# Second attention of a four-layer network: counts, maxima and scores of an iteration put in another order on three engines

## What is computed

```python
def _L1_attn_ref(x, Wq, bq, Wk, bk, Wv, bv, Wo, bo, entropy_ema, entropy_threshold):
    B, L, D = x.shape            # 8 batches of 256 tokens, width 128, 16 heads of 8
    q, k, v = (proj(Wq, bq), proj(Wk, bk), proj(Wv, bv))
    scores = jnp.einsum('bhqd,bhkd->bhqk', q, k) / jnp.float32(np.sqrt(dh))
    attn = jax.nn.softmax(scores, axis=-1)
    sr = MIN_SPARSITY + (1.0 - MIN_SPARSITY) * jax.nn.sigmoid(entropy_ema - entropy_threshold)
    k_keep = jnp.maximum(1, (L * (1.0 - sr)).astype(jnp.int32))
    rank = jnp.argsort(jnp.argsort(-attn, axis=-1), axis=-1)
    w = jnp.where(rank < k_keep[None, :, None, None], attn, jnp.float32(0.0))
    w = w / (jnp.sum(w, axis=-1, keepdims=True) + 1e-10)
    out = jnp.einsum('bhqk,bhkd->bhqd', w, v)
    return out.transpose(0, 2, 1, 3).reshape(B, L, D) @ Wo.T + bo
```

## Time and profile before

| | |
|---|---|
| median of 3 runs | 2033.48 us (2032.08 to 2033.51) |
| the profiled execution | 2029.82 us, its span 2028.1 us |
| busy share of the span | PE 77%, DVE 73%, ACT 55%, POOL 43% |
| second attention, from 480 to 1098 us | 618 us, with DVE busy 538 us, ACT 518 us, PE 421 us, POOL 270 us |

### The profile page before, as it was taken

One profiled execution on the slowest core, in us unless ns is written; L12 is line 12 of the kernel. 1 busy time (PEld: TensorE's weight loads), 2 busy tenths in 40 slices (PEclk: granted clock), 3 DMA queues, 4 the chain that ended last, 5 costly groups with the idle time before them and its releaser, 6 DMA issues.

```text
span 2028.1 us, 38143 instructions
## 1 busy us (share of the span) xinstructions
PE 1561.3 (77%) x12256; PEld 997.2 (49%) x12256; DVE 1480.3 (73%) x4763; ACT 1123.5 (55%) x3354; POOL 877.5 (43%) x1162
## 2 busy tenths in 40 slices
PE   3878989987347777776669788527777799999978
PEld 3445667675223343343336556313443477777763
DVE  6678766555589999999998742458876778887657
ACT  2444444445988998999853333114452377666620
POOL 3333221124244554455333677666200377767610
PEclk8889999997567877878778989758896899999969
DMA  4111101003000000000001033222120000000000
GB/s 139 47 47 43 41 19 43 19 2 123 15 9 17 13 10 12 17 9 9 1 1 59 31 89 106 90 70 69 47 89 1 15 1 1 2 1 2 1 1 21
DMA packets 67303, 67.53 MB, mean 33 GB/s; under 512 B 9956, under 2 KB 58967, under 8 KB 66567
## 3 DMA queue, kind: packets, MB, share of 16 engines
q1 hardware_dynamic: 58930, 53.09, 8.0%
q0 software_dynamic: 5120, 10.50, 2.0%
q10 hardware_dynamic: 3040, 1.38, 0.2%
HBM read 30.41 MB, written 8.39 MB: 19 GB/s over the span
## 4 chain that ended last, share of the span: by engine, by line
PE 35%; ACT 22%; DVE 20%; issue 9%; POOL 6%; SPq 4%; ACTq 2%; DMA 1%; DVEq 0%; POOLq 0%; another core or an unknown queue 0%
ACT rope_s L4263 5%; ACT rope_c L4263 5%; POOL weights L1170 4%; SPq L694 4%; DVE weights L3176 3%; PE bank L2163 3%; PE bank L1556 3%; PE bank L2123 3%; ACT big L4485 3%; PE bank L1572 3%; DVE nmax L2731 2%; PE bank L2150 2%; PE bank L2111 2%; ACTq L4096 2%; DVE nmax L3092 2%
## 5 line engine op out<-in xcount | busy, mean ns | idle before, releaser
L2731 DVE TENSOR_REDUCE nmax<-bank 128x4 f32<-128x1024 f32 x144 | 175.9, 1222 | 51.5 <-PE bank L1336 48.4
L1762 PE MATMUL bank<-probsT,V 128*9 128x256 f32 x512 | 156.3, 450 | 28.4 <-ACT probsT L4274 28.3
L896 POOL TENSOR_TENSOR big<-big,rinv 128x512 f32<-128x512 f32 x128 | 131.6, 1048 | 45.7 <-DVE rinv L3795 45.7
L4078 ACT ACTIVATE feat_o<-bank 128x1024 f32<-128x1024 f32 x72 | 73.7, 1023 | 103.4 <-PE bank L1336 75.4
L4078 ACT ACTIVATE O<-bank 128x1024 f32<-128x1024 f32 x72 | 73.7, 1024 | 98.5 <-PE bank L1336 71.8
L3789 DVE TENSOR_REDUCE nmax<-bank 128x2 f32<-128x512 f32 x128 | 82.0, 683 | 58.1 <-PE bank L2123 58.1
L4485 ACT ACTIVATE big<-bank,nmax 128x256 f32<-128x256 f32 x256 | 117.6, 477 | 11.1 <-DVE nmax L3789 11.1
L4493 ACT ACTIVATE big<-bank 128x512 f32<-128x512 f32 x128 | 73.8, 614 | 68.8 <-PE bank L2150 68.8
L1750 PE MATMUL bank<-silu_b,weights 128*128 128x128 bf16 x464 | 108.6, 256 | 0.0
L1170 POOL DMA_INDIRECT weights<-h_rows,V x96 | 91.7, 955 | 32.2 <-issue 28.9
L1734 PE MATMUL bank<-qT 48*128 48x256 bf16 x256 | 53.9, 346 | 62.0 <-ACT weights L4213 42.5
(11 more groups left out here) (821 smaller groups left out, 5094.5 us busy)
## 6 DMA issues: line engine op xcount, KB each, us to landing
qT<-parts SPq DMA_DIRECT2D x276, 32.0 KB
big<-V SPq DMA_DIRECT2D x192, 32.0 KB
y_rows<-weights SPq DMA_DIRECT2D x24, 256.0 KB, 2.2
big<-parts SPq DMA_DIRECT2D x180, 32.0 KB
weights<-in_weights_l_ffn SPq DMA_DIRECT2D x1, 4832.0 KB, 14.4
weights<-in_weights_l_attn SPq DMA_DIRECT2D x1, 3904.0 KB, 13.2
qT<-V SPq DMA_DIRECT2D x96, 32.0 KB
weights<-in_weights_l_ffn SPq DMA_DIRECT2D x1, 2860.0 KB, 11.4
```

The lines of the kernel that those rows point to most:

```text
L896: nc.gpsimd.tensor_tensor(row, row, rinv[:, h % H, :].unsqueeze(2).to_broadcast([P, T, S]), ALU.mult).then_inc(scaled.sem, 1)
L1762: last = mm(pb[1][part, 0:S].rearrange("p (t n) -> p t n", t=T), values_of(b, k)[:, h * wide:(h + 1) * wide], by_keys[:, k], start=k == 0, ...
L2731: V_.tensor_reduce(to, scored.rearrange("p (i a n) -> p i a n", i=HPG, n=n), AX.X, ALU.max, negate=True).then_inc(score_max.sem, 1)
L4078: nc.scalar.activation(turned_probs[n % TURNS], turned_scores, ACT.Exp).then_inc(turned_exp.sem, 1)
```

## The change

Nothing is computed in another way; four queues keep their instructions, and three of them get another order inside an iteration.

- ScalarE: the first round's counts of rows 20 to 31 stand together in front of `l1_norm(n + 3)`; before, one count stood in front of the norm and eleven behind it.
- TensorE: `l1_scores(n + 2, 0)` goes right behind `l1_doubt(n)`; `l1_turn(n + 3)` goes from in front of the scores to behind `l1_turn_probs(n, 0)`.
- VectorE, at the start: `l1_max(n + 2, 0)` goes from behind `mark(n, 0)` to between the two `largest_of` in front of the branch.
- VectorE, at the end: the maxima of heads 13, 14 and 15 stood together behind the kept counts of rows 8 to 15. Now four kept counts stand in front of each of the three.

```diff
@@ TensorE, l1_attn
                     if now(n):
                         l1_doubt(n)
+                    if now(n + 2):
+                        l1_scores(n + 2, 0)
                     if now(n - 1):
                         l1_turn_quad(n - 1, QUADS - 1)
                     if now(n + 2):
                         l1_values(n + 2)
-                    if now(n + 3):
-                        l1_turn(n + 3)
-                    if now(n + 2):
-                        l1_scores(n + 2, 0)
                         l1_scores(n + 2, 1)
                         l1_scores(n + 2, 2)
                     if now(n):
                         l1_turn_probs(n, 0)
+                    if now(n + 3):
+                        l1_turn(n + 3)
+                    if now(n):
                         l1_turn_probs(n, 1)
@@ VectorE, l1_attn
                         largest_of(n, 0)
+                    if now(n + 2):
+                        l1_max(n + 2, 0)
+                    if now(n):
                         largest_of(n, 1)
                         settle_doubt(n)
                         all_but_past(n, 0)
                         mark(n, 0)
-                    if now(n + 2):
-                        l1_max(n + 2, 0)
                     if now(n + 1):
                         first_move(n + 1)
...
                     if now(n + 1):
-                        count_kept(n + 1, 8, 16)
+                        count_kept(n + 1, 8, 12)
                     if now(n + 2):
                         l1_max(n + 2, 13)
+                    if now(n + 1):
+                        count_kept(n + 1, 12, 16)
+                    if now(n + 2):
                         l1_max(n + 2, 14)
+                    if now(n + 1):
+                        count_kept(n + 1, 16, 20)
+                    if now(n + 2):
                         l1_max(n + 2, 15)
                     if now(n + 1):
-                        count_kept(n + 1, 16, 24)
-                        count_kept(n + 1, 24, 32)
+                        count_kept(n + 1, 20, 32)
@@ ScalarE, l1_attn
                     if now(n + 1):
-                        l1_count(n + 1, 0, 20, 21)
+                        l1_count(n + 1, 0, 20, ROWS1)
                     if now(n + 3):
                         l1_norm(n + 3)
-                    if now(n + 1):
-                        l1_count(n + 1, 0, 21, ROWS1)
                     if now(n):
                         l1_take_probs(n, 0)
```

## The result

The changed kernel takes **2042.41 us** (median of 7, 2040.27 to 2049.95) against 2033.51 (7, 2028.97 to 2037.95). The medians lie 8.9 us apart; the ratio over all runs is 1.0051 [1.0039, 1.0063], some 10.4 us slower. The forecast was 2045.1, 11.6 us slower, in a range of 2039 to 2051.

The account below looks back on a forecast made before the run. DVE and ACT taking turns in a ring was taken to bound the kernel. Late maxima 9.6, first maximum before the branch 0.7 and norm round trip 1.3 gave 11.6 us slower, 2045.1 us, range 2039 to 2051.

Parts of the forecast that it names:

- The late maxima: DVE before `l1_start`: maximum 15 comes 1.60 us later, paid in six of seven starts, 9.6 us.
- the joint: At `l1_start`, ACT waits for POOL's `neg_mid`, which needs DVE's maximum 15; the wait was 0.62 us.
- Head 13's wait: ACT's exponentials of head 13 no longer wait, saving 1.49 us, but `l1_start` then waits about 3.7 us for POOL.
- The first iteration: Iteration 0: the 1.60 us vanish in ACT's 2.13 us wait for head 0's transposes, which hang on DVE alone.
- the one on POOL: POOL's candidates start 1.6 us later and were idle before and after; POOL's queue is unchanged.
- The branch: DVE's extra maximum in front of it costs 0.35 us, paid in iterations 0 and 1: 0.7 us.
- Iteration 1: DVE moves by all of 1.60 us behind the doubts' sum and ACT's wait of 0.60 us stays.
- The norm's round trip: ACT waits for PE's turning: 0.3 us in iterations 2 to 4, about 0.2 in 0 and 1; 1.3 us.
- Iterations 4 and 5: Start 1.60 us later in each, plus 0.3 us norm wait in 4; ACT's 1.07 us wait in 5 kept.
- Faster: Rival: at `l1_start`, ACT's closed bubble brings the start earlier, 10.4 us saved, 2023.1 us; chance 0.08.
- No change: Rival: the late start disappears in other waits, only 2.1 us left, 2035.6 us; chance 0.07.
- Slower still: Rival: norm round trip costs 3.3 us and the maximum before the branch 3.6, 16.5 us slower, 2050; chance 0.12.

Follow-up runs that it names:

- experiment 1: Kernel before, with only the late maxima in the new order, four kept counts in front of each of maxima 13, 14, 15: 2045.67 us, ratio 1.0056.
- experiment 3: Kernel before, with twelve kept counts instead of sixteen ahead of maxima 13 to 15: 2028.65 us, ratio 0.9971.
- experiment 4: Kernel before, with twenty-four kept counts instead of sixteen ahead of maxima 13 to 15: 2051.70 us, ratio 1.0088.
- experiment 8: Changed kernel, with VectorE's three guess instructions moved behind the next iteration's six first-round counts: 2042.98 us, ratio 1.0047 against the kernel before.
- experiment 9: Changed kernel, with VectorE's sum of doubts behind four first-round counts and its guess behind the last two: 2044.10 us, ratio 1.0059 against the kernel before.
- experiment 2: Changed kernel with the late maxima put back in their old order: 2037.66 us, ratio 1.0016 against the kernel before.
- experiment 7: Kernel before, with only head 0's scores behind the doubts' sum and their maximum in front of the branch: 2035.96 us, ratio 1.0003.
- experiment 6: Kernel before, with only the norm behind all first counts and the turning behind head 0's transposes: 2036.05 us, ratio 1.0001.
- experiment 5: Kernel before, with four kept counts fewer ahead of maxima 13 to 15 and three first-round counts moved behind the first marks: 2024.31 us, ratio 0.9941.

## Why the prediction was right, and where its steps were off

The table gives the time from one `l1_start` to the next, after minus before, in us, and what the terms of the forecast give there. The column of iteration n ends with the start in that iteration:

| iteration | -1 | 0 | 1 | 2 | 3 | 4 | 5 | 6, to the last reading | sum |
|---|---|---|---|---|---|---|---|---|---|
| forecast | 1.60 | 0.55 | 2.15 | 1.90 | 1.90 | 1.90 | 1.60 | 0 | 11.6 |
| measured | 1.60 | 1.03 | 0.96 | 1.96 | 1.69 | 2.50 | 2.53 | -0.55 | 11.72 |

**The late maxima** carried it, as forecast: 9.80 of 11.72 us in experiment 1 against a term of 9.6, and the window 15.86 against 15.85. That the sums agree so well is partly luck: this term had 1.60 in iterations -1 and 1 to 5 and nothing in 0 and 6, and experiment 1 shows, in order, 1.60, 0.94, 0.78, 1.71, 1.37, 1.73, 1.95 and -0.27. The period of iteration 2 is 71.25 us, forecast 71.2. Experiments 3 and 4 show that the joint follows maximum 15 by 1.60 us per four counts in both directions.

**Head 13's wait.** I wrote that its exponentials would not wait at all and that the start would wait 3.7 us. They wait 0.62 us for PE's L1750: their output goes into a buffer that the transposes of batch n still read. The start waits 1.49 + 0.62 + 1.60 - 0.62 = 3.09. It costs nothing here. In experiment 3 it bound, together with POOL's candidates.

**The first iteration** was to swallow all of 1.60 us, since its transposes "hang on DVE alone". In experiment 1 ACT's wait there shrank only from 2.13 to 1.51. The step that failed is the one on POOL, whose candidates "start 1.6 us later and were idle before and after": later, they run over DVE's guess, which took 1.53 us in place of 0.46 for two of its instructions in iteration 0, and DVE reached the doubts 1.17 us later (24.60 from `settle_on`, 23.43 before). That the collision stretches DVE's instructions is shown by experiments 8 and 9; that iteration 0 as a whole would be shorter without it is not, since PE took it back in experiment 9.

**The branch.** The maximum in front of it was put at 0.35 us, paid in iterations 0 and 1. In iterations 2 to 4 the way from reading to target grew by 0.16, 0.21 and 0.43 us, where the forecast has it hidden. In 0 and 1 it shrank, 4.66 to 4.53 and 5.05 to 4.78: there DVE had idled longest behind the branch, 1.65 and 2.02 us, now 0.93 and 1.18. The 0.25 us by which I let the idle time shrink were 0.45 in iteration 2.

**Iteration 1** was to take 2.15 us more and took 0.96. The branch is not the main reason, since experiment 1 leaves it alone and has 0.78. The step that failed is that DVE would move by all of 1.60 us and ACT's wait of 0.60 us stay: the doubts are read without a wait now, 0.82 us earlier behind the start, and in the change ACT's 0.60 us are gone. I had also left out a second wait of ACT in that iteration, for PE's products in front of the copy of the weighed heads. It is 0.57 us before and in experiment 2, which gained nothing there, and it is gone in the change and in experiments 1 and 7. ACT in iteration 1 of the kernel before and of experiment 1:

```profile
646.75 0.38 ACT L4278 ACTIVATE V<-bank 128x256 f32<-128x256 f32 x1 [0.57 <-PE bank L1762]
...
650.65 0.38 ACT L4283 ACTIVATE V<-bank 128x256 f32<-128x256 f32 x1
```

The last products that this copy needs took 1.60 us before, at a granted clock of 0.50, the level of 1.2 GHz, and 0.87 us in the change at 1.00, the level of 2.4 GHz. In experiment 7 the level is 1.00 there too, and iteration 1 became 0.52 us shorter without a late start. So the late start was not simply swallowed by this wait; the clock took part of it away, and why the level differs there was not tried.

**The norm's round trip** shows the waits of the forecast: 0.30 us at L1676, four times (I had said 0.2 to 0.3 in five).

**Iterations 4 and 5** took 0.6 and 0.9 us more than forecast. In the change the doubts' sum is 0.48 and 1.35 us late there (DVE waits for PE's L1779). ACT's waits there grew by 0.24 us (iteration 4) and 0.26 us (iteration 5) for PE's products in front of the copy of the weighed heads, and by 0.42 us for the transposes in iteration 5. Experiment 1 has 1.73 and 1.95 us in these two, and experiment 7 alone 0.98 us more in iteration 5, so more than one part of the change may have a share in it; which was not separated. That the excess here and in iteration 0 cancels with what iterations 1 and 6 saved is luck of the sum, not a merit of its terms.

**The rivals.** "Faster" falls with experiment 1. The Trainium skill (page "Perfetto Trace Analysis", section "Optimizing Scalar/DVE Operations") says that breaking up instructions may let work complete sooner where VectorE is not saturated but leaves bubbles. Its condition is not met in front of the start, where DVE is busy 13.92 of 14.25 us; breaking up the group of maxima there cost 0.56%, because only maximum 13, which the joint does not need, ended sooner. "No change" falls with the ratio and with the table, where seven of the eight stretches grew. "Slower still" falls with experiments 6 and 7: stretches of 1.95 and 1.11 us more, where it had 3.3 and 3.6.

## What to carry to other kernels

Before work is interleaved to feed a waiting engine sooner, find the joint that this engine comes to next: if it needs the last of the group, only the amount in front of the last counts, and closing the bubble ahead of it buys nothing. When work leaves such a joint, follow it to where it lands; by the stretches, experiment 3 got 2 of the 10 us that the joint held (5.9 us by the times), and the rest came only when the marks behind it were moved up in experiment 5. Of a transfer of work or a start that moves, ask also what it now runs beside on the other engines.

## What was unexpected of the hardware

- Small f32 instructions of VectorE took longer beside GpSimd's products of 1.16 us each: 0.19 to 0.21 us became 0.69 to 0.70, 0.27 became 0.84 to 0.85 and 0.19 became 1.08, ending as a product ended. The kept counts beside the same products kept their 0.40 us, and the instruction that reads PSUM its 0.19. The Trainium skill, page "SBUF — State Buffer", section "Who interferes with whom", calls the port pair that the two engines share an exclusive lock; the rows agree.
- The maximum in front of this kernel's branch was mostly free: 0.60 us of work changed the way from the reading to the target by -0.27 to 0.43 us in iterations 0 to 4, and the idle time behind the branch fell from between 1.15 and 2.02 us to between 0.74 and 1.18.
